# One block for both attention stages of a four-layer graph kernel, and four more ring slots

## The reference, cut to what matters

```python
q_att = jnp.einsum('nhd,rhde->rnhe', q, relation_att)
v_msg = jnp.einsum('nhd,rhde->rnhe', v, relation_msg)
aw_q_edge = q_att[etype, col_idx]
msg_edge = v_msg[etype, row_idx]
attn_score = jnp.sum(aw_q_edge * k[row_idx], axis=-1)
score = attn_score * (relation_pri[etype] / SQRT_DK)
m = jax.ops.segment_max(score, col_idx, num_segments=n)
ex = jnp.exp(score - m[col_idx])
denom = jax.ops.segment_sum(ex, col_idx, num_segments=n)
alpha = ex / denom[col_idx]
agg = jax.ops.segment_sum(alpha[..., None] * msg_edge, col_idx, num_segments=n)
```

## Time and profile before

| | us |
|---|---|
| median of 3 runs (4199.71 to 4203.07) | 4201.42 |
| the profiled execution's own time | 4203.95 |
| its span, first to last instruction | 4202.1 |
| PE busy in the span | 3172.8 (76%) |
| DVE busy | 2231.3 (53%) |
| ACT busy | 894.9 (21%) |
| POOL busy | 2744.3 (65%) |

### The profile page before, as it was taken

One profiled execution on the slowest core, in us unless ns is written; L12 is line 12 of the kernel. 1 busy time (PEld: TensorE's weight loads), 2 busy tenths in 40 slices (PEclk: granted clock), 3 DMA queues, 4 the chain that ended last, 5 costly groups with the idle time before them and its releaser, 6 DMA issues. The chain is left out here.

```text
span 4202.1 us, 64286 instructions
## 1 busy us (share of the span) xinstructions
PE 3172.8 (76%) x11666; PEld 2176.1 (52%) x11666; DVE 2231.3 (53%) x7567; ACT 894.9 (21%) x2584; POOL 2744.3 (65%) x2879
## 2 busy tenths in 40 slices
PE   5999938877788873886888878888886777676764
PEld 2444426666566642333676767777544444444442
DVE  8200047666666645344888857766663443433435
ACT  1333300000200000441444555555320000100000
POOL 3777767777677774334777747777317777477774
PEclk9999969889899986997878768777898877888776
DMA  4333323333333334566555535555313333333332
GB/s 141 141 148 146 145 71 105 106 106 105 95 106 106 106 107 145 224 246 231 165 164 165 165 94 161 163 162 163 82 46 105 105 105 105 99 105 106 106 105 90
DMA packets 226896, 540.00 MB, mean 129 GB/s; under 512 B 73482, under 2 KB 107948, under 8 KB 212876
## 3 DMA queue, kind: packets, MB, share of 16 engines
q0 software_dynamic: 136528, 374.97, 30.3%
q1 hardware_dynamic: 57880, 103.46, 6.8%
q10 hardware_dynamic: 32164, 57.91, 4.6%
HBM read 390.04 MB, written 146.09 MB: 128 GB/s over the span
## 5 line engine op out<-in xcount | busy, mean ns | idle before, releaser
L579 POOL DMA_INDIRECT gcn_edges_g<-table,rows_i x782 | 741.1, 948 | 429.4 <-ACTq L844 191.8
L892 PE MATMUL ps<-gcn_edges_g,gcn_edges_onehot 128*128 x1760 | 627.6, 496 | 308.5 <-SPq L590 274.5
L937 DVE TENSOR_TENSOR acc<-acc,ps 128x256 f32 (+1 forms) x880 | 369.4, 420 | 751.9 <-PE ps L892 740.4
L892 PEld LDWEIGHTS ps<-gcn_edges_g,gcn_edges_onehot 128*128 128x128 f32 x1760 | 391.0, 242 | 537.6 <-issue 484.3
L305 POOL DMA_INDIRECT records<-rec,slots x391 | 376.2, 962 | 184.7 <-issue 124.0
L579 POOL DMA_INDIRECT sum_g<-table8v,rows_i x391 | 379.7, 971 | 163.0 <-issue 112.2
L579 POOL DMA_INDIRECT rel_g<-table,rows_i x391 | 372.1, 952 | 135.0 <-issue 96.9
L579 POOL DMA_INDIRECT score_g<-table8k,rows_i x391 | 371.3, 950 | 135.1 <-issue 112.7
L579 POOL DMA_INDIRECT conv_edges_g<-table,rows_i x391 | 371.6, 950 | 127.4 <-issue 93.8
L357 PE MATMUL ps<-w,xt 128*128 128x512 f32 x1000 | 435.8, 595 | 18.3 <-ACT xt L327 18.3
L1016 PE MATMUL ps<-q,onehot_t 128*128 x880 | 320.5, 500 | 113.2 <-DVE onehot_t L1114 111.9
(11 more groups left out here) (315 smaller groups left out, 4778.5 us busy)
## 6 DMA issues: line engine op xcount, KB each, us to landing
table<-tb SPq DMA_DIRECT2D x50, 1280.0 KB, 4.5
score_dst_bc<-dst_rows ACTq DMA_DIRECT2D x110, 256.0 KB, 3.5
sum_dst_bc<-dst_rows ACTq DMA_DIRECT2D x110, 256.0 KB, 3.5
gcn_edges_g<-table,rows_i POOLq DMA_INDIRECT x782
table<-gcn_tb SPq DMA_DIRECT2D x50, 128.0 KB, 1.7
records<-rec,slots POOLq DMA_INDIRECT x391
rel_g<-table,rows_i POOLq DMA_INDIRECT x391
conv_edges_g<-table,rows_i POOLq DMA_INDIRECT x391
```

The costliest lines, as they stand in the source:

```text
L579: pool.indirect_dma_start(out=m.g[:, 2 * (p % RING) + j, 0:D], out_offset=None, in_=table, in_offset=bass.IndirectOffsetOnAxis(ap=m.rows_i ...
L892: mm = pe.matmul(bank(m, i % BANKS, 0, width), m.onehot[:, 2 * k + j, :], window(m.g, slot + j, 0, width), start=(j == 0), stop=(j == 1))
L937: nc.vector.tensor_tensor(acc, acc, bank(m, i % BANKS, 0, width), ALU.add).then_inc(added, 1)
```

## The change

The ring gets four slots more (`SLOTS` = 20): pairs 192 to 195 go to slots 16 to 19 instead of 0 to 3, and POOL no longer waits for a release before them. So slots 0 to 15 are free of the last four pairs, and the next stage's pairs 0 to 15 can use them as the pairs 176 to 191 are given back. `attention_scores` and `attention_sum` no longer open blocks: each returns its five streams, and the new `attention_edges` puts them into one block, on each engine the scores' stream and behind it the sums'. Both use one buffer `m.g` (the sums' instructions therefore read `score_g` by name). The sums' gathers wait, for the first 16 pairs, for what the scores have given back (`ahead_of`), and SP gives back all the scores' pairs (`to_the_end`). DVE waits for the last maximum before it starts the sums. The clearing block moves behind the sums, and the sums' own semaphores are now cleared too.

```diff
+LAST_PAIRS = PAIRS % RING
+SLOTS = RING + LAST_PAIRS
...
-    m.g = ctx.enter_context(nc.sbuf_tensor(f"{stage}_g", [P, 2 * RING, ACCW], F32))
+    m.g = ctx.enter_context(nc.sbuf_tensor(f"{stage}_g", [P, 2 * SLOTS, ACCW], F32))
...
+def slot_of(p):
+
+    return p % RING if p < PAIRS - LAST_PAIRS else RING + p - (PAIRS - LAST_PAIRS)
...
-def gather_all(pool, m, table, rows):
+def gather_all(pool, m, table, rows, ahead_of=None):
+
 
     for p in range(PAIRS):
-        if p >= RING and p % 2 == 0:
-            pool.wait_ge(m.released, p + 2 - RING)
+        if p % 2 == 0:
+            if RING <= p < PAIRS - LAST_PAIRS:
+                pool.wait_ge(m.released, p + 2 - RING)
+            elif ahead_of is not None:
+                pool.wait_ge(ahead_of, min(PAIRS - LAST_PAIRS - RING + p + 2, PAIRS))
...
+    if to_the_end:
+        for p in range(PAIRS - RELEASE_LAG, PAIRS):
+            release(p)
...
+            nc.vector.memset(m.g[:, 2 * SLOTS - 1, 0:D], 0.0)
...
+    def sync(sp):
+        use_gather(m, gather)
+        relay_pairs(sp, m, multiplied, UNROLL, to_the_end=True)
...
+    def gpsimd(pool):
+        use_gather(m, gather)
+        gather_all(pool, m, m.table8v[0:ROWS * RELS8, :], ROWS8, ahead_of=scores_released)
...
+    def vector(dve):
+        use_gather(m, gather)
+        dve.wait_ge(maxed, ITEMS)
+        dve.sem_inc(multiplied, UNROLL)
+        dve.sem_inc(diff_ready, 2)
+        dve.sem_inc(added, UNROLL)
...
         @block.gpsimd
         def _(pool):
-            gather_all(pool, m, m.table8k[0:ROWS * RELS8, :], ROWS8)
+            scores[1](pool)
+            sums[1](pool)
...
-                nc.vector.tensor_copy(m.cols16[:, :], m.iota_i[:, :])
                 nc.vector.tensor_copy(m.item_ids[:, :], ids_i[:, :])
...
-        attention_scores(nc, m)
+        attention_edges(nc, m)
```

More of the change, by code:

```diff
@@ L524, in edge_buffers, with use_gather @@
     m.gather_stages += 1
+    return m.arrived, m.released, m.gather_stages
+def use_gather(m, gather):
+    m.arrived, m.released, m.gather_stages = gather
+def slot_of(p):
+    return p % RING if p < PAIRS - LAST_PAIRS else RING + p - (PAIRS - LAST_PAIRS)
 def gathered_before(m, k):
-    pairs = len(range(k, PAIRS, RING))
-    lost = (TILES - USED) if k == (PAIRS - 1) % RING else 0
+    pairs = PAIRS // RING if k < RING else 1
+    lost = (TILES - USED) if k == slot_of(PAIRS - 1) else 0
     return 16 * (2 * pairs - lost) * (m.gather_stages - 1)
 def gathered_by(m, p):
-    tiles = sum(min(2, USED - 2 * q) for q in range(p % RING, p + 1, RING))
-    return gathered_before(m, p % RING) + 16 * tiles
+    if p >= PAIRS - LAST_PAIRS:
+        return gathered_before(m, slot_of(p)) + 16 * min(2, USED - 2 * p)
+    return gathered_before(m, p % RING) + 32 * (p // RING + 1)
 class ItemRegisters:
@@ L579, in gather_all, with relay_pairs, release @@
             pool.indirect_dma_start(
-                out=m.g[:, 2 * (p % RING) + j, 0:D], out_offset=None, in_=table,
+                out=m.g[:, 2 * slot_of(p) + j, 0:D], out_offset=None, in_=table,
                 in_offset=bass.IndirectOffsetOnAxis(ap=m.rows_i[:, rows, t:t + 1], axis=0)
-            ).then_inc(m.gathered[p % RING], 16)
-def relay_pairs(sp, m, consumed, ahead):
+            ).then_inc(m.gathered[slot_of(p)], 16)
+def relay_pairs(sp, m, consumed, ahead, to_the_end=False):
+    def release(p):
+        items = sp.value_load(m.release[0:1, bass.ds(p, 1)], min_val=1, max_val=ITEMS)
+        sp.wait_ge(consumed, items + ahead)
+        sp.sem_inc(m.released, 1)
     def pair(p, k, by, releases):
@@ L591, in pair @@
         if releases:
-            items = sp.value_load(m.release[0:1, bass.ds(p - RELEASE_LAG, 1)], min_val=1, max_val=ITEMS)
-            sp.wait_ge(consumed, items + ahead)
-            sp.sem_inc(m.released, 1)
+            release(p - RELEASE_LAG)
     for k in range(RING):
@@ new lines, in sb @@
+    def sb(name, shape, dt=F32):
+        return ctx.enter_context(nc.sbuf_tensor(name, shape, dt))
+    dst_bc = sb("score_dst_bc", [P, SPREADS, 2 * P])
+    onehot_t = sb("onehot_t", [P, 2, 2 * P])
+    prod = sb("prod", [P, 2, 2, D])
+    near_t = sb("near_t", [P, 2, P])
+    steps = sb("steps", [P, 2, P + 1])
+    gaps = sb("gaps", [P, 2, P])
+    runs = sb("runs", [P, 2, P])
+    tops = sb("tops", [P, 2, P])
+    topx = sb("topx", [P, 2, 2 * BATCH, HEADS + 1])
+    absent = sb("absent", [P, 2, 2 * BATCH])
@@ L1099, in _ @@
+            scores[3](act)
+            sums[3](act)
         @block.vector
         def _(dve):
[L1102 to L1108 removed]
@@ L1335, in layer_norm @@
+            scores[4](dve)
+            sums[4](dve)
 def layer_norm(nc, m, stage, prepare, out):
@@ L2074, in four_graph_layers @@
         m.ident = sb("ident", [P, P])
-        m.lower = sb("lower", [P, P])
-        m.cols16 = sb("cols16", [P, P], I16)
-        m.item_ids = sb("item_ids", [1, ITEMS])
         m.items = sb("items", [1, ITEMS, 4], U16)
@@ L2135, in four_graph_layers @@
         m.bias = sb("bias", [P, 3, D])
-        m.gathered = sems(ctx, nc, "all", *(f"gathered{k}" for k in range(RING)))
+        m.gathered = sems(ctx, nc, "all", *(f"gathered{k}" for k in range(SLOTS)))
         m.gather_stages = 0
```

675 lines of the change are left out of this document (340 added, 335 removed).

## The result

The changed kernel takes 4174.43 us (median of 6 runs, 4170.29 to 4177.06) against 4200.69 (6 runs, 4198.14 to 4203.07) on the same chip: a ratio of 0.9937, interval 0.9924 to 0.9949, 26 us less. Predicted were 4175.3, with a range of 4163 to 4189. The profiled execution's own time is 4177.06, its span 4175.2.

A forecast was written before the change was run, and what follows sets the result against it. POOL's own gather pace was taken to bound both attention stages. Last gather 31.5 us earlier, clears 5.5 lost, small parts 0.1 won: 26.1 less than 4203.95 is 4177.9, and 2.5 lower for the median, 4175.3; range 4163 to 4189.

The forecast's parts named there:

- The pace and the hole: Between scores and sums: POOL, pacing both stages, fills 43.9 us without gathers; 32 go out, the 33rd could start at 2481.7.
- The eight waits at nothing: Before the sums' first gathers: POOL's eight waits on the scores' releases cost nothing.
- the stand: Before the sums' 33rd gather: POOL stands still because the ring is full, 13.0 us, from 2481.7 to 2494.7.
- The new wait: Sums' 33rd gather waits for two pairs back, until 2494.7, with 4.3 us of the turn after the last maximum gone.
- To the end: Rest of the sums: 358 gathers at 1.276 us, the last at 2951.5 against 2983.0, 31.5 us earlier.
- The clears: Behind the sums: 76 clears, at most 0.072 us each, delay DVE's biases; 5.5 us lost, lower bound 4.4.
- rival 4: Sums: TensorE stays at 1.2 GHz, so PE bounds the stage; 74 us slower, 4275; chance 3%.
- rival 2: Sums: consumers sink behind the full ring for several stretches at the lower clock, eating part of the gain; 4193; chance 5%.
- 3 fell: End of the scores: maxima each wait for a whole gather, so sums begin 33 us later; 7 us slower, 4208; chance 3%.
- 5 fell: Turn to the sums: a wait of POOL or SP holds the gathers until the last maximum; 4202.5; chance 4%.
- Rival 1: Sums: POOL gathers at the scores' faster pace, 1.254 us; 7.9 us more gain, 4167; chance 17%.

The follow-up runs named there:

- Experiments 1 and 3: Changed kernel with scores and sums in two blocks again: 4199.85 us, ratio 1.0002; changed kernel with POOL waiting for the last maximum before the sums' gathers: 4197.36, 1.0000.
- Experiment 2: Changed kernel, still one block, but with the ring of 16 slots as before instead of 20: 4174.41 us, ratio 0.9947.
- experiment 6: Changed kernel with 61 of the 76 clears done by SP within the joint block, on a slower chip: 5458.59 us, ratio 0.9994.
- Experiment 7: Changed kernel with the weights of DVE's weighing read from PSUM: 5477.38 us, ratio 1.0027, on a slower chip; 4170.05, 0.9926, on one like the first.
- experiments 5 to 8 and 10: 8: changed kernel, sums' fifth pair waits for last maximum, 1.0017 and 1.0022. 10: changed kernel, clears hidden, weights in PSUM, ACT's transfers and table load earlier, 0.9997.
- experiment 5: The changed kernel itself again, on a chip where the kernel before takes 5461.0 us: 5465.07 us, ratio 1.0010.
- ring20: Changed kernel with its 20 slots used as a plain ring of 20 pairs in all stages: 4174.44 us, ratio 0.9945.

## Why the prediction was right

*The pace and the hole.* The step on which all rests, that POOL's own pace bounds both stages, held: idle before the first gather of the sums 0.31 us (0.3 predicted), and the 32nd started at 2481.43, so that the 33rd could have followed at 2482.7. Predicted was 2481.7; the scores ended 1.0 us later in this execution. Experiments 1 and 3 show that the hole is the whole gain.

*The eight waits at nothing.* Held: POOL passed all of them without a stop. Experiment 2 shows what one would cost, 4.40 us, and that the stand behind it would have swallowed most of it.

*The new wait.* 13.0 us predicted up to 2494.7; the gather started at 2494.63 after 12.25 us idle, of which 0.3 are its usual gap. The part of the turn that was taken as gone was right: from the last maximum to the second addition 14.30 us instead of 18.59, 4.29 less (4.3 predicted), and the first mask waited 4.34 us (4.4 predicted). That even the start agrees to 0.1 us is luck in part: the last gather of the scores was 1.0 us later than before, and the last maximum stood 38.8 us behind it instead of 40.0.

*To the end.* Last gather 2951.5 predicted, 2952.7 measured: the pace behind the 33rd was 1.2794 us, not 1.276, and 358 times 0.0034 is the 1.2. The backlog was worked off by some 120 us, as the 10-us windows show (columns as in rows 1): PE at the higher clock with work in hand, then the swings of before.

```profile
2504.00:2514.00 10.00, 8.76 (x48) 7.52 (x48) 9.03 (x37) 7.06 (x28) 7.74 (x8) 1.00 0.60 162
...
2604.00:2614.00 10.00, 7.81 (x46) 6.90 (x44) 8.32 (x33) 7.11 (x29) 7.57 (x9) 1.00 0.61 184
...
2634.00:2644.00 10.00, 8.13 (x31) 6.89 (x30) 5.96 (x25) 4.96 (x20) 7.57 (x8) 0.69 0.53 158
```

What follows the last gather, up to the end of the last addition, was to stay at 8.1 us and took 7.1.

*The clears.* Mis-sized, within its bounds: 5.5 us lost predicted, with 0.072 a clear; DVE waits 4.90 us, 4.6 more than before, and a clear costs 0.056 (experiment 6).

*How near the sum came.* In the spans, 4202.1 and 4175.2, the gain is 26.9 us, and the pieces give it: 30.3 for the last gather, 1.0 behind it, less 4.6 for the clears. Predicted were 26.1. The pace was 1.2 us against the forecast, the end of the stage and the clears 1.0 and 0.9 in its favour. So the mechanism was right, but that the median came out within 1 us of the forecast owes something to errors that cancel, and is finer than the scatter of single executions (4170 to 4177).

*The rivals.* The mean clock of the sums rose from 0.76 to 0.81 (rival 4 fell), no wait over 0.3 us came later (2 fell), the maxima took 164 ns in the middle (3 fell), the queue ran on (5 fell). Rival 1 did not happen by the change: the pace was 1.279. Most of the difference between the two stages, though, is now explained (17 of some 25 ns a gather), and by something that was in the text under another head: the rule of the Trainium skill, "SBUF — State Buffer", section "Who interferes with whom", that a DVE instruction with two inputs in SBUF contends with a GpSimd one that reads SBUF. I weighed it against the maxima, where the rows spoke against a loss, and not against the weighing, which also has two such inputs and comes 220 times in this stage. Experiment 7 agrees with it in one direction: gathers that start while a weighing runs take 1047 ns, and 945 without its second SBUF input. It does not bear out what the prediction took from there, that whoever comes second waits for the whole of the other: a weighing that starts inside a gather takes its usual 426 ns. The maxima fit this: 27 of the last 41 start inside a gather, and they lost nothing.

*What the sum did not hold.* It holds for a chip on which POOL binds. On the two others of experiments 5 to 8 and 10 the condition was not met. There the same program gained nothing (experiment 5): the consumers bound the stage, which rival 2 had only for a few stretches.

## What to carry to other kernels

Where one queue issues at a fixed pace through two stages, ask only how long it stands between them, and then how many of its items the buffer takes before someone gives one back: the gain is the hole less the stand at the full ring. A barrier that keeps a producer from work that doesn't need the result is worth its hole less that stand (here 43.9 us less 12.0, of which the clears behind the sums took 4.6 back), and extra buffers are worth nothing until the stand, not the barrier, is the limit. Before counting on it, see that the producer's waits are its own in the profile; on a chip where they are releases, the same edit gives nothing.

## What was not expected

- The same program takes 4200 us on some chips and 5460 on others, and the verdict on the change depends on it (0.9937 and 1.0010).
- POOL needs 4.60 us from the end of its last gather to the meeting of the engines, the same at three stage ends of the kernel before and of the changed one; in ring20 it was 7.2; in sixteen_slots one such end, that of the joint block, came 9.2 us behind.
- A second exponential on ACT into PSUM, 0.16 us an item, costs the item's chain nothing that can be seen (14.36 and 14.30 us). With the weights read from there, the mean gather is 17 to 28 ns shorter, and only the gathers that start during a weighing change.
